# A chunked recurrence on one core: order of TensorE's and VectorE's work around the scans

## The chip, the cores and the metric

The kernel runs on one core of a Trainium2 chip. Its time is the device time of one execution in microseconds, and the number quoted for a kernel is the median of its runs. The profile is of one execution on the same core, with its own time. The engines are TensorE (PE, its weight loads PEld), VectorE (DVE), ScalarE (ACT), GpSimd (POOL) and SyncE (SP, which starts DMAs). They run side by side, each works through its own list in order, and they meet in semaphores.

## The reference

One block of a hybrid network over 2048 tokens of 256 numbers: a gated recurrence with rotations, a mixture of 8 experts, a windowed attention, and the mixture again. The change lies in the recurrence alone:

```python
q = causal_conv(ln(x) @ Wq); k = causal_conv(ln(x) @ Wk); v = causal_conv(ln(x) @ Wv)   # 4 taps each, 6 heads of 64
theta = q[..., ::2] * inv_freq; psi = k[..., ::2] * inv_freq
alpha = sigmoid(ln(x) @ Wa); beta = sigmoid(ln(x) @ Wb)
state = rotate(state, theta_t - theta_(t-1)) * alpha + beta * rotate(v, psi)            # over the tokens
out   = rotate(state, -theta)
g = ln(x) @ Wg
o = out * rsqrt(mean(out**2) + eps) * rms_w * silu(g)
x = x + o @ Wo
```

Turning the state into a frame that rotates with theta makes the recurrence a plain scan, `o = alpha * o + w`, with `w` the values turned by the angle psi - theta and scaled by beta.

## The kernel before, in words

The recurrence works on four chunks of 512 tokens. Features lie on the partitions, tokens along the row. All engines run one loop over the chunks, `it` = 0 to 3, and in turn `it` the outputs of chunk `it` are finished while chunk `it + 1` (`ahead`) is prepared up to its scans. What stands ahead of the loop prepares chunk 0. So there are three full turns, and a last one with outputs alone.

Preparing a chunk means, on TensorE: `angles` for two units of 128 features (24 matmuls of 512 columns each, L351, the taps folded into the weights), `decays` (six matmuls to 12 rows), three value projections and three gate projections (`value_or_gate`, six matmuls each, L362), then `betas` and `alphas` (L386 to L394), which spread the decays over the partitions. Angles, values and gates share one PSUM tensor of two banks, `psV`; each projection waits until ScalarE has copied out the one that held its bank. ScalarE rounds the angles (`rounded`, L515), VectorE subtracts (`start`, L675), and only then may values overwrite the bank. ScalarE copies values out (`values_out`, L529), takes sines (`turns`), and Silu of the gates (L544). VectorE convolves the values with four taps (`taps`, L725 for the first and L729 for the others), turns them (`rotate`), adds (`write`), scales by beta (`write_scaled`), and runs three scans (`scans`, L762), which start from the carried state `carry` of the chunk before (L765).

Finishing a chunk means: ScalarE squares the scans' outputs (L550), TensorE sums the squares by head (`squares`, 24 small matmuls to 6 columns, L403), ScalarE adds a constant (`means`, L555), GpSimd raises to the power -1/2 (`deviations`, L632, two instructions), TensorE spreads the result over the partitions (`rms_spread`, L413), VectorE multiplies it with the gated outputs (`outputs`, L777 and L774; the gating is GpSimd's, L625), and TensorE projects (`project_out`, L425). In the turn after that the result is added to x and normalised (`tail_stats_dve`, `tail_xn_dve`, with GpSimd's part `tail_pool`, TensorE's transposes L162 and ScalarE's copy), the logits of the experts follow (`routed_logits`, L997), VectorE picks two experts per token (`Routing`, in two parts: up to the picks, L1057 to L1076, and from the counts on, L1093 to L1113), TensorE counts (`pe_ranks`, which waits for the picks, L1023), and GpSimd sends the rows out (L1184). The first turn has no logits and picks; instead the last chunk's input is transposed and split into high and low parts there (L147), and the first projection waits for that split.

Nothing but the order of the calls in each engine's list sets the order of the work. After the four turns a barrier closes the recurrence (L180), and experts and attention follow in blocks of their own.

## Time and profile before

| | us |
|---|---|
| median of the runs | 772.26 (767.83, 772.26, 773.0) |
| profiled execution | 766.56 |
| its span, first to last instruction | 764.8 |
| TensorE busy | 618.8 (81%) |
| VectorE busy | 465.6 (61%) |
| ScalarE busy | 296.7 (39%) |
| GpSimd busy | 342.0 (45%) |

The shares are over the whole program. What concerns the recurrence is read from its own stretch, which ends 229 us into the span, by the timeline of each engine and by stretches cut at points of TensorE's order.

### The profile page before, as it was taken

The page shows a single profiled execution, that of the slowest core. Times are in us where ns is not written, and L with a number is a line of the kernel's source. Part 1 is how long each engine was busy: PE and PEld are TensorE (multiplying, and loading weights), DVE is VectorE, ACT ScalarE, POOL GpSimd, SP SyncE. Part 2 cuts the span into 40 slices and gives each one's busy share as a digit, 9 for nine tenths or more (in the row PEclk, how much of TensorE's full clock was granted, in tenths as well). Part 3 has the DMA queues.
Part 4 walks back from the last instruction along what each step waited for, and adds up shares of the span by engine and source line. Part 5 has one row for each costly group of instructions (what it writes and reads, how often), then busy time and mean ns, then how long its engine had stood idle before and what let it go on. Part 6 is the DMA issues. An engine that isn't in the chain of part 4 may idle for free. (4 is left out here: it accounts for less than half of the span.)

```text
span 764.8 us, 14771 instructions
## 1 busy us (share of the span) xinstructions
PE 618.8 (81%) x4827; PEld 479.8 (63%) x4827; DVE 465.6 (61%) x1226; ACT 296.7 (39%) x567; POOL 342.0 (45%) x400
## 2 busy tenths in 40 slices
PE   1789999995639999964569999999988769999950
PEld 0667787774535767743457787877866545777740
DVE  6994858869435534456365766787786544644422
ACT  1363435152002444444134545555454413444420
POOL 4304040723531667755332444345557650653435
PEclk9998989896666999986658999999999756999985
DMA  8599500132011453327435246403501512443328
GB/s 274 201 351 351 184 1 0 45 90 74 22 61 56 145 168 98 100 79 239 62 69 85 57 105 150 95 24 78 107 17 46 135 53 58 145 135 100 99 93 295
DMA packets 68318, 86.94 MB, mean 114 GB/s; under 512 B 8909, under 2 KB 62802, under 8 KB 67380
## 3 DMA queue, kind: packets, MB, share of 16 engines
q1 hardware_dynamic: 61428, 67.80, 32.7%
q0 software_dynamic: 6816, 18.19, 6.7%
q8 instruction: 42, 0.69, 0.4%
q14 instruction: 32, 0.26, 0.1%
HBM read 35.13 MB, written 39.06 MB: 97 GB/s over the span
## 5 line engine op out<-in xcount | busy, mean ns | idle before, releaser
L1295 POOL DMA_INDIRECT back<-f_yout,f_target x78 | 76.9, 985 | 113.2 <-ACT f_yout L1402 102.6
L1337 PE MATMUL bank<-f_wgu,f_xt 128*128 x312 | 113.5, 488 | 3.4 <-ACT f_xt L1387 3.3
L1184 POOL DMA_INDIRECT xs<-xn,f_slots x64 | 65.2, 1018 | 57.3 <-ACT xn L1175 41.7
L1442 DVE TENSOR_TENSOR f_hid<-f_act_g,bank 128x176 f32<-128x176 f32 x78 | 26.4, 338 | 104.3 <-ACT f_act_g L1394 100.2
L1359 PE MATMUL bank<-f_wd,f_hT 88*128 x312 | 81.5, 385 | 0.0
L2069 POOL TENSOR_SCALAR_AFFINE_SELECT b_prob<-b_prob 128x512 f32<-128x512 f32 x60 | 38.4, 640 | 92.6 <-ACT b_prob L2310 92.3
L2310 ACT ACTIVATE b_prob<-bank 128x1024 f32<-128x1024 f32 x60 | 61.5, 1024 | 46.2 <-PE bank L2149 45.9
L1337 PEld LDWEIGHTS bank<-f_wgu,f_xt 128*128 128x128 f32 x312 | 59.2, 199 | 31.1 <-issue 9.4
L2379 DVE COPY_PREDICATED bank<-b_later,bank 128x512 f32<-128x512 int32 x60 | 41.6, 694 | 33.5 <-PE bank L2119 30.1
L1359 PEld LDWEIGHTS bank<-f_wd,f_hT 88*128 88x128 f32 x312 | 54.2, 193 | 4.8
L1402 ACT ACTIVATE f_yout<-bank,f_share 128x256 f32<-128x256 f32 x78 | 37.0, 474 | 39.8 <-PE bank L1359 38.9
L1394 ACT ACTIVATE f_act_g<-bank 128x176 f32<-128x176 f32 x78 | 24.8, 318 | 66.7 <-PE bank L1337 66.7
L2190 PE MATMUL bank<-b_prob,b_V 128*17 128x128 f32 x992 | 42.0, 288 | 9.1 <-POOL b_prob L2071 8.5
L2383 DVE TENSOR_REDUCE b_m<-bank 128x4 f32<-128x512 f32 x64 | 44.2, 691 | 8.2 <-PE bank L2110 6.1
L2071 POOL TENSOR_SCALAR_AFFINE_SELECT b_prob<-b_prob 128x512 f32<-128x512 f32 x64 | 41.0, 641 | 11.5 <-ACT b_prob L2307 11.5
L2149 PE MATMUL bank<-b_QS,b_KS 64*128 64x128 f32 x496 | 41.5, 276 | 1.0 <-ACT b_prob L2310 0.7
L1387 ACT ACTIVATE f_xt<-bank 128x256 f32<-128x256 f32 x78 | 30.0, 384 | 25.9 <-PE bank L1321 17.6
L2149 PEld LDWEIGHTS bank<-b_QS,b_KS 64*128 64x128 f32 x496 | 36.5, 192 | 3.2 <-ACT b_prob L2310 2.0
L2119 PE MATMUL bank<-b_KS,b_QS 48*128 48x256 f32 x208 | 30.8, 343 | 8.1 <-DVE b_m L2383 8.1
L351 PE MATMUL bank<-xTh,wfh 128*128 128x512 f32 x64 | 30.1, 470 | 8.3 <-DVE wfl L705 8.3
L2190 PEld LDWEIGHTS bank<-b_prob,b_V 128*17 128x17 f32 x992 | 22.3, 99 | 20.8 <-POOL b_prob L2071 16.6
L1321 PE MATMUL bank<-ident_sb,f_xin 128*128 128x128 f32 x156 | 32.0, 289 | 1.4 <-DMA f_xin<-xs 1.4
(313 smaller groups left out, 1475.4 us busy)
## 6 DMA issues: line engine op xcount, KB each, us to landing
xs<-xTf SPq DMA_DIRECT2D x8, 2176.0 KB, 19.2
f_xin<-xs SPq DMA_DIRECT2D x78, 136.0 KB, 2.1
f_wgu<-in_wgu SPq DMA_DIRECT2D x4, 1408.0 KB, 6.0
f_wgu<-back SPq DMA_DIRECT2D x16, 256.0 KB, 5.6
b_KS<-b_kh SPq DMA_DIRECT2D x32, 128.0 KB, 4.1
b_QS<-b_qh SPq DMA_DIRECT2D x32, 128.0 KB, 3.8
f_back<-back SPq DMA_DIRECT2D x8, 512.0 KB, 8.5
f_wd<-in_wd SPq DMA_DIRECT2D x4, 968.0 KB
```

The source lines that it names most:

```text
L1184: pool.indirect_dma_start(m.xs, bass.IndirectOffsetOnAxis(m.slots[:, g, c, i:i + 1], 0), xn[:, g * TPC + i], None)\
L1295: pool.indirect_dma_start(m.back, bass.IndirectOffsetOnAxis(target[:, g % AR:g % AR + 1], 0), yout[:, g % YB], None, bounds_check=2 * 2 * ...
L1337: mm = pe.matmul(psG[:, g % 2, 0:2 * FH], xt[:, g % 2, k * P:(k + 1) * P], m.gu[:, k, bass.ds(e, 2 * FH)], start=k == 0, stop=k == KD - 1)
L1359: mm = pe.matmul(psY[:, g % 2, 0:D], hT[:, g % 2, k * P:(k + 1) * P], m.wd[:, k, bass.ds(e, D)], start=k == 0, stop=k == 1)
L1402: act.activation(yout[:, g % YB], psY[:, g % 2, 0:D], ACT.Copy, scale=share[:, g % AR:g % AR + 1])\
L2069: pool.affine_select(halves_of[:, :, 0], halves_of[:, :, 0], [[0, 4], [-1, P]], ALU.is_gt, 0.0, base=0, channel_multiplier=1)
L2071: pool.affine_select(halves_of[:, :, 1], halves_of[:, :, 1], [[0, 4], [1, P]], ALU.is_ge, 0.0, base=0, channel_multiplier=-1).then_inc(kep ...
L2149: mm = pe.matmul(own_t[:, half, i, w], KS[rows, 2 * u + i, ring(b - 1 + w)], QS[rows, 2 * u + i, ring(b)], start=True, stop=True)
L2190: mm = pe.matmul(psO[CG * j:CG * j + HV1, u * P:(u + 1) * P], V[:, (b - 1 + w) % RING, 4 * u + j], prob[:, quad(b, u) % 2, half, c:c + P], ...
L2310: ins = act.activation(dst, psT[:], ACT.Exp, scale=SCALE)
L2379: dve.copy_predicated(own_s[:, :, :, 1], later[:].unsqueeze(1).unsqueeze(1).broadcast_to([P, 2, 2, P]), own_s[:, :, :, 0]).then_inc(sel_do ...
L2383: dve.tensor_reduce(mo[:, :, 2 * u:2 * u + 2], own_s[:, :, :, 1], AX.X, ALU.max).then_inc(m_done, 1)
```

## The change

On TensorE, both angle units of the next chunk come before the squares, and its three values directly behind them; two of the three gates come before the projection. On ScalarE, copying the carried state is new work behind the squares; the rounding of the next angles moves ahead of the means, the values' copies ahead of the transposed rows, and of the three gates one precedes the copy of the counts. On VectorE, the copy of the carried state is gone, the taps run value by value instead of tap by tap and stand before the outputs instead of behind them (the last tap no longer behind the picks), `start` precedes the normalisation, and `rotate` follows the picks instead of the second part of the routing. GpSimd's list and the DMAs keep their order.

```diff
@@ -468,9 +468,11 @@
                     ahead = it + 1 < NCH
                     if ahead:
                         angles(it + 1, 0)
+                        angles(it + 1, 1)
                     squares(it)
                     if ahead:
-                        angles(it + 1, 1)
+                        for i in range(VT):
+                            value_or_gate(it + 1, i)
                     if it == 0:
                         first_transposed(3)
                     else:
@@ -480,17 +482,15 @@
                     rms_spread(it, 0)
                     if ahead:
                         rms_spread(it, 1)
-                        value_or_gate(it + 1, 0)
-                        value_or_gate(it + 1, 1)
-                        value_or_gate(it + 1, 2)
                     if it > 0:
                         routed_logits(it - 1)
                     if ahead:
+                        value_or_gate(it + 1, VT)
+                        value_or_gate(it + 1, VT + 1)
                         project_out(it)
                         if it > 0:
                             pe_ranks(pe, m, 0, it - 1, psB[:, 0])
-                        for i in range(VT, NVG):
-                            value_or_gate(it + 1, i)
+                        value_or_gate(it + 1, VT + 2)
                         if it > 0:
                             pe.wait_ge(m.route, routed(0, it - 1, COPIED))
                         betas(it + 1)
@@ -537,9 +537,13 @@
                     act.activation(angle[:, 0], angle[:, 0], ACT.Sin, scale=-TWO_PI)
                     act.activation(angle[:, 1], angle[:, 1], ACT.Sin, scale=sscale[:, 0:1]).then_inc(sin_ready, 1)
 
-                def gates(it):
+                def carried(it):
+                    act.wait_ge(scan_done, now(it, GT, GT))
+                    act.activation(carry[:], o[:, :, CH - 1], ACT.Copy).then_inc(carry_done, 1)
+
+                def gates(it, which=range(VT, NVG)):
                     act.wait_ge(o2_ready, before(it, NOUT, NOUT))
-                    for i in range(VT, NVG):
+                    for i in which:
                         act.wait_ge(vg_ready, now(it, i + 1, NVG))
                         act.activation(gate[:, i - VT], psV[:, i % 2], ACT.Silu).then_inc(vg_out, 1)
 
@@ -575,9 +579,12 @@
                 gates(0)
                 for it in range(NCH):
                     squares(it)
+                    if it + 1 < NCH:
+                        carried(it)
+                        rounded(it + 1)
                     means(it)
                     if it + 1 < NCH:
-                        rounded(it + 1)
+                        values_out(it + 1)
                     if it == 0:
                         tail_act(act, t0, 3)
                     else:
@@ -586,12 +593,12 @@
                         tail_rows_act(act, tl, it - 1)
                     if it + 1 < NCH:
                         sigmoids(it + 1)
-                        values_out(it + 1)
                         turns(it + 1)
+                        gates(it + 1, [VT])
                     if it > 0:
                         act_counts(act, m, 0, it - 1, psB[:, 0])
                     if it + 1 < NCH:
-                        gates(it + 1)
+                        gates(it + 1, range(VT + 1, NVG))
                     if it > 0:
                         act_tanh(act, m, xn, 0, it - 1)
                 tail_rows_act(act, tl, NCH - 1)
@@ -717,18 +724,18 @@
                     dve.tensor_tensor(wgl[:], wg_raw, wgh[:].bitcast(F32), ALU.subtract).then_inc(wgl_done, 1)
                     dve.tensor_tensor(wof[:], wo_raw, rmsw[:].unsqueeze(2).broadcast_to([P, GT, D]), ALU.mult).then_inc(wgl_done, 1)
 
-                def taps(it, j):
-                    for i in range(VT):
+                def taps(it, i):
+                    for j in range(TAPS):
                         src = vraw[:, i, PAD - TAPS + 1 + j:PAD - TAPS + 1 + j + CH]
                         if j == 0:
                             dve.wait_ge(vg_out, now(it, i + 1, NVG))
                             dve.tensor_scalar(vconv[:, i], src, convv[:, i, 0:1], None, ALU.mult)\
                                .then_inc(tap_done, 1)
                         else:
-                            dve.wait_ge(tap_done, now(it, (j - 1) * VT + i + 1, NTAP))
+                            dve.wait_ge(tap_done, now(it, i * TAPS + j, NTAP))
                             dve.scalar_tensor_tensor(vconv[:, i], src, convv[:, i, j:j + 1], vconv[:, i],
                                                      ALU.mult, ALU.add).then_inc(tap_done, 1)
-                    if j == TAPS - 1:
+                    if i == VT - 1:
                         dve.tensor_copy(vraw[:, :, 1:PAD], vraw[:, :, CH + 1:CH + PAD]).then_inc(halo_done, 1)
 
                 def rotate(it):
@@ -761,9 +768,8 @@
                     for g in range(GT):
                         dve.tensor_tensor_scan(o[:, g], psF[:, g // 2], w[:, g], carry[:, g:g + 1],
                                                ALU.mult, ALU.add).then_inc(scan_done, 1)
-                    dve.wait_ge(scan_done, now(it, GT, GT))
-                    dve.tensor_copy(carry[:], o[:, :, CH - 1]).then_inc(carry_done, 1)
                     if it == NCH - 1:
+                        dve.wait_ge(scan_done, now(it, GT, GT))
                         dve.wait_ge(vg_out, now(it, NVG, NVG))
                         dve.tensor_tensor(gate[:], gate[:], o[:], ALU.mult).then_inc(gated, GT)
 
@@ -799,8 +805,8 @@
                 tail_xn_dve(dve, t0, 3)
                 tail_split_dve(dve, t0, 1)
                 dve.wait_ge(wgl_done, 2)
-                for j in range(TAPS):
-                    taps(0, j)
+                for i in range(VT):
+                    taps(0, i)
                 rotate(0)
                 write(0)
                 write_scaled(0)
@@ -811,26 +817,27 @@
                         tail_split_dve(dve, t0, 2)
                     else:
                         tail_stats_dve(dve, tl, it - 1, add=True)
-                        tail_xn_dve(dve, tl, it - 1)
                     if ahead:
                         start(it + 1)
+                    if it > 0:
+                        tail_xn_dve(dve, tl, it - 1)
                     if it == 0:
                         m.prepare(dve, xn)
+                    if ahead:
+                        for i in range(VT):
+                            taps(it + 1, i)
                     outputs(it, 0)
                     if ahead:
                         outputs(it, 1)
                     if it == 0:
                         tail_split_dve(dve, t0, 3)
-                    if ahead:
-                        for j in range(TAPS - 1):
-                            taps(it + 1, j)
                     if it > 0:
                         group = Routing(dve, m, 0, it - 1)
                         group.take(psB[:, 0, LOGITS])
                         group.compare()
                         group.choose()
                     if ahead:
-                        taps(it + 1, TAPS - 1)
+                        rotate(it + 1)
                     else:
                         outputs(it, 1)
                     if it > 0:
@@ -839,7 +846,6 @@
                         group.difference()
                         group.payload(xn)
                     if ahead:
-                        rotate(it + 1)
                         write(it + 1)
                         write_scaled(it + 1)
                         scans(it + 1)
```

How that stands in the lists, first on TensorE, around the squares (L403) of the second turn; L351 is an angle matmul, L362 with `wvh` and `wvl` one of a value, and the weights `wfh` and `wfl` are the high and low halves. Before:

```order
L351 MATMUL bank1<-xTl,wfh 128x512
L403 MATMUL bank2<-headsum,sq 128x6 x12
L351 MATMUL bank1<-xTh,wfh 128x512
L351 MATMUL bank1<-xTh,wfl 128x512
L351 MATMUL bank1<-xTl,wfh 128x512
```

And with the change:

```order
L351 MATMUL bank1<-xTl,wfh 128x512
L403 MATMUL bank2<-headsum,sq 128x6 x12
L362 MATMUL bank1<-xTh,wvh 128x512
L362 MATMUL bank1<-xTh,wvl 128x512
L362 MATMUL bank1<-xTl,wvh 128x512
```

The 24 matmuls of the second angle unit have moved from behind the squares to ahead of them, and the values now follow the squares with nothing in between.

On VectorE, the second turn from the end of the scans (L762) to the picks (L1076; with the change the line numbers are a few higher). Before:

```order
L765 COPY carry<-o 128x3
L130 TENSOR_TENSOR x_tok<-bank,x_tok 128x1024
L133 BN_STATS stats<-x_tok 128x6 x4
L136 BN_AGGR meanvar<-stats 128x2 x4
L142 TENSOR_SCALAR xn<-x_tok,meanvar,rstd 128x256 x4
L675 SCALAR_TENSOR_TENSOR angle<-whole,bank 128x1024
L777 TENSOR_TENSOR sq<-gate,bank 128x1024
L774 TENSOR_TENSOR sq<-gate,bank 128x512
L725 TENSOR_SCALAR vconv<-vraw,convv 128x512 x3
L729 SCALAR_TENSOR_TENSOR vconv<-vraw,convv,vconv 128x512 x6
L1057 COPY f_L<-bank 128x32
```

And with the change:

```order
L136 BN_AGGR meanvar<-stats 128x2 x4
L682 SCALAR_TENSOR_TENSOR angle<-whole,bank 128x1024
L142 TENSOR_SCALAR xn<-x_tok,meanvar,rstd 128x256 x4
L732 TENSOR_SCALAR vconv<-vraw,convv 128x512
L736 SCALAR_TENSOR_TENSOR vconv<-vraw,convv,vconv 128x512 x3
...
L739 COPY vraw<-vraw 128x3x3
L783 TENSOR_TENSOR sq<-gate,bank 128x1024
L780 TENSOR_TENSOR sq<-gate,bank 128x512
L1063 COPY f_L<-bank 128x32
```

The pair L732 and L736 stands there three times in a row, once per value; the dots stand for its second and third time. All twelve taps and the copy of the last columns (L739) now precede the outputs (L783, L780), and the picks begin behind those.

## Rows read from the trace of the kernel before

**Rows 1.** Stretches between the alphas' ends: bounds and length in us, engines' busy times, TensorE's clock.

```profile
core 0: us, PE busy (x) PEld busy (x) DVE busy (x) ACT busy (x) POOL busy (x), PEclk, DMA share, GB/s
53.30:92.89 39.59, 37.92 (x220) 29.88 (x219) 26.55 (x38) 15.98 (x21) 9.54 (x6) 0.91 0.95 294
92.89:134.37 41.48, 39.57 (x243) 31.54 (x242) 29.76 (x60) 16.59 (x24) 10.82 (x8) 0.92 0.00 1
134.37:178.03 43.66, 40.11 (x243) 31.74 (x242) 34.36 (x63) 16.58 (x24) 19.39 (x17) 0.92 0.27 72
```

**Rows 2.** Waits of TensorE, 53 to 187 us: total, times, longest.

```profile
PE bank L403 <- ACT sq L550: 9.6, 3, 7.2
PE bank L1023 <- DVE f_pick L1076: 2.6, 2, 1.3
PE bank L362 <- ACT gate L544: 1.9, 3, 0.6
```

**Rows 3.** Stretches of TensorE alone: length, busy time, granted clock, DMA.

```profile
60.06:63.74 3.68, 3.56 (x24) 0.84 1.13 350
63.74:71.95 8.21, 8.21 (x25) 0.66 1.13 352
92.89:100.11 7.22, 7.22 (x25) 0.76 0.00 0
100.11:102.71 2.60, 2.60 (x26) 1.00 0.00 0
102.71:109.92 7.21, 7.21 (x27) 0.76 0.00 1
134.37:140.20 5.83, 5.83 (x25) 1.00 0.20 75
141.68:145.26 3.58, 3.40 (x24) 0.89 0.22 80
145.26:153.66 8.40, 8.40 (x26) 0.64 0.00 0
```

**Rows 4.** Timeline: the carry copy in two turns, and GpSimd's gating beside the first.

```profile
142.51 3.72 POOL L625 TENSOR_TENSOR gate<-gate,o 128x512 f32<-128x512 f32 x3
143.28 2.98 DVE L765 COPY carry<-o 128x3 f32<-128x3 f32 x1
...
186.99 0.17 DVE L765 COPY carry<-o 128x3 f32<-128x3 f32 x1
```

**Rows 5.** First taps and fold products (ns min/median/max, first and last start); GpSimd's subtraction.

```profile
L725 DVE TENSOR_SCALAR vconv<-vraw,convv x12: 486/486/900, 40.8 to 163.0; 128x512 f32<-128x512 f32 x12
...
L695 DVE TENSOR_TENSOR f_wgu<-f_wgu,w x2: 693/1225/1757, 11.6 to 12.2; 128x512 f32<-128x512 f32 x2
...
40.18 1.28 POOL L619 TENSOR_TENSOR sgl<-sg,sgh 12x512 fp32r<-12x512 f32 x1 [1.60 <-ACT sgh L523]
```

**Rows 6.** Timeline of GpSimd, first turn: the power for the scales.

```profile
64.29 4.52 POOL L632 TENSOR_TENSOR rms<-ms,minus_half 128x16 f32<-128x16 f32 x2 [1.23 <-ACT ms L555]
```

**Rows 7.** Timeline of VectorE: outputs and split (first turn), taps and routing (second).

```profile
75.46 1.22 DVE L777 TENSOR_TENSOR sq<-gate,bank 128x1024 f32<-128x1024 f32 x1 [0.51 <-PE bank L413]
...
77.20 1.22 DVE L147 TENSOR_TENSOR xTl<-bank,xTh 128x1024 fp32r<-128x1024 f32 x1
...
116.56 0.49 DVE L725 TENSOR_SCALAR vconv<-vraw,convv 128x512 f32<-128x512 f32 x1 [1.31 <-ACT vraw L529]
...
119.68 4.06 DVE L729 SCALAR_TENSOR_TENSOR vconv<-vraw,convv,vconv 128x512 f32<-128x512 f32 x6
123.66 0.18 DVE L1057 COPY f_L<-bank 128x32 f32<-128x32 f32 x1
...
126.83 2.08 DVE L729 SCALAR_TENSOR_TENSOR vconv<-vraw,convv,vconv 128x512 f32<-128x512 f32 x3
```

**Rows 8.** Timeline of TensorE, second turn: first value matmul, logits, projection.

```profile
114.17 0.50 PE L362 MATMUL bank<-xTh,wvh 128*128 128x512 f32 x1
...
118.45 1.85 PE L997 MATMUL bank<-f_wr_raw,xTf 128*128 128x8 f32 x16
...
120.15 5.43 PE L425 MATMUL bank<-wof,sq 128*128 128x256 f32 x24
```

## The prediction, written before the run

> **What bounds the kernel now.** I read the table of stretches first. The recurrence fills the first 229 of 764.8 us; the change touches nothing behind it, and a barrier separates the two, so what the last chunk's scans gain arrives at the end of the program unchanged. Cut at the end of the alphas' matmuls, the three full turns of its loop take 39.59, 41.48 and 43.66 us, and TensorE is busy in 37.92, 39.57 and 40.11 of them; VectorE in 26.6 to 34.4 [rows 1]. So TensorE's order bounds the loop, and VectorE follows it. What is not plain matmul work on TensorE has two sources.
>
> First, its waits [rows 2]: 9.6 us for the squares, of which 7.2 lie behind the last turn, so 2.4 here; 2.6 for the routing's picks; 1.9 for a gate's bank. In the chunks whose squares arrive one by one the 24 small matmuls of that step take 3.68 and 3.58 us against 2.60 when all three are there [rows 3]: 2.1 more. Second, the granted clock. Twenty-four angle matmuls take 5.83 us at the full level (2.4 GHz), 5.6 up to the start of what follows, since the last one overlaps with it. Four stretches were partly at the lower level (1.2 GHz): 8.21, 7.22, 7.21 and 8.40 us at a mean clock of 0.66, 0.76, 0.76 and 0.64 [rows 3]. Three of them follow the squares, one the betas and alphas. They cost 2.6 + 1.6 + 1.6 + 2.8 = 8.6 us. Waits, slow squares and clock together are 2.4 + 2.6 + 1.9 + 2.1 + 8.6 = 17.6 us of the three turns.
>
> **The change part by part.** *TensorE.* Both angle units now run before the squares, 11.2 us of dense work. A turn's scans end 8.9 us behind the alphas (178.03 in [rows 1], 186.99 in [rows 4]), so the squares are all there: the 2.4 and the 2.1 go. Two gates move ahead of the projection and only the third follows; the picks and the gate's bank are then ready behind 5.4 us of projection [rows 8]: the 2.6 and the 1.9 go. The clock's 8.6 I count anew below.
>
> *Carry copy to ScalarE.* On VectorE it took 2.98 us in one chunk and 0.17 when nothing ran beside it [rows 4]. It is off the path: behind it VectorE waited in every turn for ScalarE's rounding, which waited for the angles on TensorE. On ScalarE it stands behind the squares and ahead of that same wait. Counted 0; should the angles stop being late, it is worth up to 2.8 us once.
>
> *ScalarE's and GpSimd's other steps.* The means wait for the squares on TensorE wherever they stand; the transposed rows give way to the three values' copies, and the logits that need them come 5 us later on TensorE; sines and the first gate follow while VectorE still has taps, outputs and picks to do. Counted 0; without that cover a late sine holds the rotation, which is the second rival. GpSimd's list keeps its order; where its sends stand ahead of the gating (from 142.51, when the scans were nearly over [rows 4]) the power may begin up to 1 us later, which goes into the range. SyncE's loads of expert weights wait for the last angles and values and start some us earlier, with nobody waiting: 0.
>
> *Taps by value.* Taps that don't depend on each other start every 0.66 us (4.06 for six less 2.08 for three, over three) though each lasts 0.76 [rows 7]. By value each waits for the one before, so nine cost at least 0.76 each, 6.8 us, and the three first ones 0.49 each [rows 5]: 8.3 us. That is about 0.8 more per chunk, and is in the chain below. The three chunks' extra increments and the tap order of chunk 0, ahead of the loop, I count as 0: VectorE's next work there waits for betas and alphas on TensorE.
>
> *A new wait.* Here is the step that decides. Before, the taps came long after GpSimd's power for the scales; now the values follow the squares directly on TensorE, and ScalarE has the first one out about 2.4 us after them (values start at 114.17 on TensorE, the first tap at 116.56; [rows 7, 8]). GpSimd's power starts 0.55 us behind the squares (63.74 in [rows 3], 64.29 in [rows 6]) and lasts 4.52, to 5.1 us behind them. The first tap of a value is a one-input VectorE operation like the carry copy, and both wait for GpSimd: the carry copy issued at 143.28, inside GpSimd's three products, ended at 146.26, with the last of them at 146.23 [rows 4]; the first tap that met GpSimd's 1.28 us subtraction at 40.18 took 0.90 instead of 0.49 [rows 5]. So I let the first tap wait for the whole power. The bounds are no wait (2.4 us) and the whole of it (5.1 us); the carry copy is the nearest row, and I take 5.1.
>
> From the end of the squares, VectorE then needs 5.1 + 8.3 + 0.2 (halo) + 1.7 (outputs, 75.46 to 77.20) = 15.3 us until the outputs are written, and in the first turn 1.2 more, since the projection also waits for the last split [rows 7]. TensorE is at the projection after the values 4.3, transposes, decays and the spread of the scales 4.25 (109.92 to 114.17), logits 1.7 and two gates of 1.43, a third of the values' time, = 13.1 us, in the first turn 11.4 without logits [rows 3, 8]. **It waits 5.1, 2.2 and 2.2 us, 9.5 in all.** A slow clock behind the squares, 1.6 to 2.8 us as before, fits into these waits and costs nothing on top. That is the trade: the old stalls give way to one before the projection.
>
> The Trainium skill, page "SBUF — State Buffer", section "SBUF: two separate sides", speaks against the change here too, but more mildly: such a VectorE operation and a GpSimd instruction lock each other out for one whole instruction. This trace shows more than that: the carry copy stayed out over three GpSimd instructions in a row. By the page the tap would come in between the two power instructions and the sum would be about 4.5 us better, 762, the first rival below; I go by the row.
>
> *Clock, what stays.* Waiting 5 us before the first projection probably lowers the clock under it. Bounds: 0, and 2.6 as for the angles behind the idle and squares of the first turn; I take 1.5. One fall behind betas and alphas in three turns, as before: 1.6 (bounds 0 and three at 1.6).
>
> *Sum.* Removed 17.6; added 9.5 + 1.5 + 1.6 = 12.6; the last alphas end 5.0 us earlier. From the outputs to the end of the scans VectorE needs 19.6 us (123.66 to 143.28) less three taps and the halo, 2.1 = 17.5 [rows 4, 7]. From the projection to the alphas TensorE needs 14.2 (120.15 to 134.37) less the 1.9 of waits and two gates 2.9 = 9.4 [rows 1, 8]. The scans thus end 8.1 behind the alphas, against 8.9: another 0.8. **Gain 5.8 us.** Behind the scans the order is as before. The profiled execution, 766.56 us, becomes 760.8. The runs shown are 767.83, 772.26 and 773.0, so the profiled one lies 5.7 under their median; I take the median's side: 772.26 - 5.8 = **766 us** (766.46, rounded down). By the runs' own spread, 1% (7.7 us) is about what a measurement of this kernel can tell from no change.
>
> **Rivals.** *The taps don't wait, or less.* If the first tap comes in between the power's two instructions, of which the second handles 8 of 24 columns and so takes about a third, an estimate of 1.5 us, the waits shrink by 1.5 in each turn: 766 - 4.5 = 762. With no wait at all VectorE is done at 12.5 us, TensorE never waits outside the first turn, and the clock may hold: 17.6 and 0.8 gained and about 2 added, 756. For it: operations with two inputs did get in between GpSimd's products, 1.76 us against 0.69 alone [rows 5]. Against it: the carry copy did not. Chance 0.25.
>
> *It is all given back.* VectorE's work from the squares to the outputs is longer than I count (the subtraction on GpSimd, 1.28 us, falls among the taps and holds one of them; ScalarE's sines come late for the rotation), by some 2 us a turn: 766 + 6 = 772. For it: VectorE has no slack left in that stretch. Chance 0.20.
>
> *Slower: the cold projection.* In each turn the wait before the projection lets the clock fall, and projection, gate, betas and alphas hold it down into the next angles. That makes 2.7 of cold angles and 1.5 of cold projection three times, 12.6 instead of the 3.1 I counted; 9.5 more: 766 + 9.5 = 776, and with the projections at their bound of 2.6 each 779. It decides where the wait is long enough for a fall in all three turns, not in the first alone. For it: betas and alphas preceded a fall once (92.89 in [rows 3]) without any long wait. Against it: the turn with 1.28 us of waiting before the picks shows no fall behind its alphas (134.37, clock 1.00), and what comes before the projection is dense. Chance 0.10.
>
> The forecast has what is left, 0.45. Its own range is 763 to 770 by the bounds of clock and first wait. For 8 in 10 I go from 758, inside the case without waits, to 774, inside the given-back case and noise of the median. Faster by over 1% means under 764.5: the first rival and a part of the forecast, 0.25 + 0.09 = 0.34. Slower by over 1% means over 780: the third rival's end together with the runs' spread, 0.06. Within 1%: 0.60.
>
> **What would show it.** In the profile after: squares in 2.6 us with no wait before them; the first tap of each chunk starting where the power on GpSimd ends, or, if that step is wrong, some 2.4 us behind the squares; TensorE's idle before the projection 5, 2 and 2 us, named after the outputs on VectorE; no idle before picks and gates; the scans of the last chunk at 181 instead of 187. Taps at 0.77 to 0.79 us a step. Wrong would be angles at a mean clock under 0.8 in all turns, or VectorE idle before the rotation for the sines.

## The result and the profile after

The changed kernel takes 757.61 us (756.68 to 759.75, four runs) against 770.35 us of the kernel before in four (767.83, 768.44, 772.26, 773.0), 12.7 us between the medians. A ratio, here and below, is taken from runs in the faster of two states alone, so it need not be the quotient of the medians (0.983): it is 0.988, interval 0.9835 to 0.9929. That is 1.2% faster, just past the 1% that the prediction called "within", and the median lies 0.4 us below the low end of its range. With more runs (12 and 23, first experiment on the other parts) the ratio is 0.992 (0.987 to 0.997), 6.2 us less on 770.62, close to the 5.8 us forecast. By these the size was met. The way to it was not: the step on which the sum turned did not happen.

The profiled execution took 759.75 us, its span is 758.0 us, 6.8 shorter than the one before. First the stretches between the alphas' ends (as in [rows 1]: length, busy times of the engines, TensorE's clock):

```profile
55.61:96.65 41.04, 37.91 (x219) 30.05 (x219) 27.52 (x36) 16.19 (x22) 9.82 (x6) 0.91 0.85 265
96.65:134.75 38.10, 37.98 (x243) 30.59 (x243) 29.41 (x56) 16.40 (x23) 11.06 (x8) 0.96 0.00 1
134.75:172.86 38.11, 37.95 (x243) 30.55 (x242) 32.84 (x62) 16.90 (x25) 19.98 (x16) 0.96 0.32 82
```

The three turns take 117.25 us instead of 124.73. In the second and third TensorE is idle for 0.1 to 0.2 us: nothing but its own work sets them. TensorE's waits from 53 to 187 us, beside [rows 2]:

```profile
PE bank L403 <- ACT sq L554: 6.6, 1, 6.6
PE bank L425 <- issue: 3.1, 1, 3.1
PE bank L425 <- DVE sq L780: 0.2, 1, 0.2
```

Those for picks and for a gate's bank are gone, the 6.6 for the squares lie behind the last turn. In front of the projection (L425) stands 3.1 us in the first turn and 0.2 behind, where the sum had 5.1, 2.2 and 2.2. TensorE alone (as in [rows 3]):

```profile
55.61:68.78 13.17, 13.17 (x50) 0.84 1.13 352
68.78:71.49 2.71, 2.71 (x26) 1.00 1.13 351
...
86.16:92.92 6.76, 6.76 (x25) 0.75 0.09 28
96.65:109.44 12.79, 12.79 (x49) 0.87 0.00 0
...
134.75:147.54 12.79, 12.79 (x49) 0.87 0.18 67
```

The rows are: both angle units of the first turn, its squares, its projection, and the angles of the second and third turn. Squares now take 2.7 us in each turn, without a wait (predicted 2.6). The angles (11.26 us for both units at the full level, shown below) lose 1.9, 1.5 and 1.5 us to the low clock, and the projection loses 1.7 (5.07 at the full level, below). And the step itself, on GpSimd and VectorE in the second turn:

```profile
112.58 4.72 POOL L639 TENSOR_TENSOR rms<-ms,minus_half 128x16 f32<-128x16 f32 x2 [6.78 <-ACT ms L559]
121.15 1.29 POOL L626 TENSOR_TENSOR sgl<-sg,sgh 12x512 fp32r<-12x512 f32 x1 [3.86 <-ACT sgh L523]
...
114.52 0.49 DVE L732 TENSOR_SCALAR vconv<-vraw,convv 128x512 f32<-128x512 f32 x1 [1.22 <-ACT vraw L529]
115.04 2.33 DVE L736 SCALAR_TENSOR_TENSOR vconv<-vraw,convv,vconv 128x512 f32<-128x512 f32 x3
...
120.56 3.22 DVE L736 SCALAR_TENSOR_TENSOR vconv<-vraw,convv,vconv 128x512 f32<-128x512 f32 x3
...
123.77 1.21 DVE L783 TENSOR_TENSOR sq<-gate,bank 128x1024 f32<-128x1024 f32 x1
```

The squares end at 112.15. The first tap starts at 114.52, 2.4 us behind them, in the middle of the power, and takes its usual 0.49; it had waited for ScalarE's copy of the value alone. The three taps behind it, with two inputs each, take 2.33 us inside the power. The third value's three taps take 3.22 us, beside GpSimd's subtraction; so it is in all three turns of this trace.

### The profile page after: what moved, and what is told of

Read it like the earlier page. It is cut to its first block and busy times, and to the rows that moved or that the text cites. A ratio compares the mean times of both kernels' runs of the same rounds, so it can differ in the third digit from the quotient of the medians.

```text
span 758.0 us, 14773 instructions
## 1 busy us (share of the span) xinstructions
PE 617.0 (81%) x4827; PEld 479.6 (63%) x4827; DVE 467.2 (62%) x1222; ACT 297.2 (39%) x570; POOL 343.8 (45%) x400
## 5 line engine op out<-in xcount | busy, mean ns | idle before, releaser
L2077 POOL TENSOR_SCALAR_AFFINE_SELECT b_prob<-b_prob 128x512 f32<-128x512 f32 x64 | 40.9, 639 | 11.5 <-ACT b_prob L2313 11.5
L351 PE MATMUL bank<-xTh,wfh 128*128 128x512 f32 x64 | 28.6, 446 | 8.3 <-DVE wfl L712 8.3
L1353 PEld LDWEIGHTS bank<-ident_sb,f_hid 128*88 128x88 f32 x156 | 19.3, 125 | 21.6 <-issue 13.7
```

Of the source, the lines that this page charges most:

```text
L2077: pool.affine_select(halves_of[:, :, 1], halves_of[:, :, 1], [[0, 4], [1, P]], ALU.is_ge, 0.0, base=0, channel_multiplier=-1).then_inc(kep ...
```

## How the experiments are read

Where a kernel has six executions or more, they scatter by 11 to 20 us, and go with the mean granted TensorE clock that each lists: of 80 runs of the kernel before, the slowest has 779.31 us at 0.847 and the fastest 759.51 at 0.879. A line through all runs, with a constant for each kernel, falls by 4.9 us for 0.01 of clock and leaves 1.4 us. So the table gives, beside the median and the ratio to before on the same chip, the difference to before at equal mean clock, from that line and all runs, with its 95%. What an order gains or loses by raising or lowering the mean clock itself is not in that difference; whether any does was not separated (median clocks of the changed kernel and of before, first experiment on the other parts: 0.865 and 0.859). The other columns come from one trace each: the three turns between alphas, and TensorE's waits in them. The two kernels with probes or products ran once each, for their traces (770.51 and 778.52 us).

| kernel | median (runs) | ratio | at equal clock | turns | waits |
|---|---|---|---|---|---|
| before, second trace | 769.44 (8) | 0.999 (0.992 to 1.006) | 0 | 121.71 | 5.8 |
| changed, again | 764.22 (12) | 0.992 (0.987 to 0.997) | -4.8 ± 0.8 | 116.88 | 3.1 |
| outputs earlier, first turn | 760.13 (6), 757.03 (12) | 0.984 (0.972 to 0.995), 0.989 (0.985 to 0.993) | -9.7 ± 0.7 | 108.76, 111.74 | 0.2, 0.4 |
| outputs earlier, all turns | 758.16 (6) | 0.990 (0.981 to 0.998) | -9.1 ± 1.1 | 111.16 | 0.9 |
| carry copy on VectorE | 761.49 (12) | 0.993 (0.988 to 0.998) | -5.2 ± 0.8 | 117.36 | 3.3 |
| first tap waits | 768.71 (12) | 1.006 (1.001 to 1.011) | +3.2 ± 0.8 | 126.23 | 11.7 |
| gates late | 773.59 (6) | 1.012 (1.002 to 1.023) | +3.7 ± 1.1 | 134.25 | 14.1 |
| outputs before taps | 767.85 (12) | 0.998 (0.993 to 1.004) | -1.1 ± 0.8 | 119.81 | 8.0 |
| angles split | 777.81 (6) | 1.014 (1.003 to 1.025) | +4.6 ± 1.1 | 131.57 | 12.1 |

## Experiments on the step that failed

**The first tap made to wait.** What the prediction assumed, put in by hand:

```diff
                     if ahead:
+                        dve.wait_ge(rms_ready, now(it, NRMS, NRMS))
                         for i in range(VT):
                             taps(it + 1, i)
```

> The change with one wait added: the first tap of each chunk waits for the whole of GpSimd's power, which is the step that the prediction counted on and that the trace did not show. Theory A (the sum was right but for this step): the first tap moves from 2.4 to about 5.1 us behind the squares, TensorE's idle before the projection becomes 5.8, 2.8 and 2.8 us instead of 3.1, 0.2 and 0, and the time is 8 us above the changed kernel's at the same mean clock: nothing left of the gain, ratio to before 0.998 to 1.006. Rival B (the projection is not held by the taps): the time of the changed kernel, ratio 0.992.

The power and first tap of the first turn in that kernel, and TensorE's waits:

```profile
70.09 4.51 POOL L639 TENSOR_TENSOR rms<-ms,minus_half 128x16 f32<-128x16 f32 x2 [5.99 <-ACT ms L559]
74.64 0.49 DVE L732 TENSOR_SCALAR vconv<-vraw,convv 128x512 f32<-128x512 f32 x1 [4.68 <-POOL rms L639]
```

```profile
PE bank L425 <- issue: 5.9, 1, 5.9
PE bank L425 <- DVE sq L780: 5.8, 2, 3.0
```

The tap starts where the power ends, 5.0 us behind the squares (69.67), and the idle before the projection is 5.9 and twice 2.9, as expected. At equal clock the kernel is 8.0 us above the changed one, the ratio 1.006 at the edge of what was expected. Theory A stands: the projection hangs on the taps, and the sum's price for a held first tap was right (2.7 us a turn; the waits grow from 3.3 to 11.7). The hold was not there.

**What holds VectorE: probes.** A copy with the form of the carried state's stands ahead of the first tap, a tap-like operation where GpSimd gates; nobody reads either.

```diff
+                def probe_tap():
+                    dve.tensor_scalar(probe[:], o[:, 0], convv[:, 0, 0:1], None, ALU.mult)
+
+                def probe_copy():
+                    dve.tensor_copy(seen[:], sq[:, :, CH - 1])
...
+                    if it in (1, 2):
+                        probe_tap()
                     if ahead:
                         start(it + 1)
...
                         for i in range(VT):
+                            if i == 0:
+                                probe_copy()
                             taps(it + 1, i)
```

> The change with two probes on VectorE, whose results nobody reads: ahead of each chunk's first tap a copy of 128x3 values with the form of the copy of the carried state (so it meets GpSimd's power), and ahead of the subtraction of the angles in the second and third turn a tap-like operation (one input, 128x512; in the third turn it meets GpSimd's gating products). Theory A (what GpSimd runs decides: products of 128x512 hold VectorE out, the power on 128x24 values does not): the copy takes 0.17 to 0.2 us inside the power, the tap-like operation inside the gating takes over 1 us instead of 0.49. Rival B (what VectorE runs decides: a plain copy is held out, a tap with its scalar from memory is not): the copy inside the power takes 1.5 to 4.7 us, the tap-like operation 0.49 inside the gating.

The copy beside the power (second turn) and the tap-like operation beside the gating (third), from its timeline:

```profile
109.74 4.72 POOL L640 TENSOR_TENSOR rms<-ms,minus_half 128x16 f32<-128x16 f32 x2 [6.64 <-ACT ms L560]
110.38 0.16 DVE L746 COPY seen<-sq 128x3 f32<-128x3 f32 x1
...
142.05 3.76 POOL L633 TENSOR_TENSOR gate<-gate,o 128x512 f32<-128x512 f32 x3
143.01 3.09 DVE L743 TENSOR_SCALAR probe<-o,convv 128x512 f32<-128x512 f32 x1
```

The copy passes inside the power in 0.16 us; the tap-like operation takes 3.09 and ends behind the last product (0.46 in the second turn, outside the products). What GpSimd runs decides, not what VectorE runs: theory A. The carry copy of [rows 4] is no model for a tap beside the power, since its neighbour was another.

**Products in the power's place.** GpSimd computes three products of 128x512 into an unused place and then one product of the 128x24 values, instead of the power (so the scales are left out).

```diff
+                    if it + 1 < NCH:
+                        pool.wait_ge(wgl_done, 1)
+                        for n in range(3):
+                            pool.tensor_tensor(probe[:, n * KD:(n + 1) * KD], wgh[:, :, 0:2 * P].bitcast(F32), wgl[:, :, 0:2 * P].bitcast(F32), ALU.mult)
...
+                        if it + 1 < NCH:
+                            pool.tensor_tensor(by_h(rms), by_h(ms), by_h(minus_half), ALU.mult).then_inc(rms_ready, 1)
+                            continue
                         pool.tensor_tensor(by_h(rms), by_h(ms), by_h(minus_half), ALU.pow).then_inc(rms_ready, 1)
```

> The change with GpSimd's power replaced by three products of 128x512 values into an unused place and a product of the same 128x24 values (so the scales are not the right ones). Theory A (products of that size hold the first taps out, the power does not): the first tap, ready 2.4 us behind the squares, ends with the last of the products, some 4.4 us behind the squares, or is as long as one product, over 1 us, and TensorE's idle before the projection is 1 to 2 us longer in each turn than in the changed kernel. Rival B (the first tap gets in whatever GpSimd runs): 0.49 us at 2.4 us behind the squares, and the same idle as in the changed kernel.

First taps beside the products in the first and third turn, the normalisation beside them in the second, then TensorE's waits:

```profile
69.48 3.97 POOL L641 TENSOR_TENSOR probe<-wgh,wgl 128x512 f32<-128x512 f32 x3 [5.99 <-ACT ms L560]
71.41 0.90 DVE L740 TENSOR_SCALAR vconv<-vraw,convv 128x512 f32<-128x512 f32 x1 [2.06 <-ACT vraw L530]
...
109.33 3.40 DVE L142 TENSOR_SCALAR xn<-x_tok,meanvar,rstd 128x256 f32<-128x256 f32 x4
...
151.69 3.90 POOL L641 TENSOR_TENSOR probe<-wgh,wgl 128x512 f32<-128x512 f32 x3 [2.27 <-ACT ms L560]
...
154.36 1.52 DVE L740 TENSOR_SCALAR vconv<-vraw,convv 128x512 f32<-128x512 f32 x1
```

```profile
PE bank L426 <- issue: 4.6, 1, 4.6
PE bank L426 <- DVE sq L788: 4.1, 2, 2.1
```

The tap takes 0.90 and 1.52 instead of 0.49, the four operations of the normalisation 3.40 instead of 1.38, and TensorE idles 1.5 to 2 us longer in each turn: theory A again. Here the tap stays out for the product that runs (in the first turn it ends at 72.31, the products at 73.45); the probe above stayed out for the rest of three. The carry copy of the kernel before did both: 2.98 us in the third turn, but 0.28 and 0.34 in the first two, where it met the same three products (lines in the section on the prediction). The operations that stayed out for all (2.98, 3.09, and 2.97 in the second trace of before) are all in the third turn, where the products follow GpSimd's sends; whether that makes the difference is open.

## Experiments on the other parts

**The changed kernel again**, without an edit.

> The changed kernel once more, five rounds. Theory A (the gain is made in the three full turns, whose stretches shrank from 124.73 to 116.99 us, and TensorE's order sets it): 757 to 758 us, ratio about 0.983 to 0.988; in an execution whose gates of the first chunk, ahead of the loop, run at the high clock, the first alphas end at 53.3 instead of 55.6 us and the gain of the loop shows whole. Rival B (a good part of the 12.7 us between the medians is the difference between executions and not the change): ratio 0.99 or above.

The ratio, 0.992, is rival B's, its interval reaches down into theory A's. The turns, 116.88 us, are those of the first trace (117.25), as theory A has it; but part of the 12.7 us was the executions', as rival B has it. The first four runs of the changed kernel had clocks of 0.873 to 0.877; here its median clock is 0.865. The trace, of an execution with a mean clock of 0.849, shows the low clock elsewhere than in the first one; the rows are the first turn's angles and projection, the angles of the second turn, its values, the angles of the third, its values:

```profile
55.83:69.66 13.83, 13.83 (x50) 0.79 1.13 352
87.05:92.12 5.07, 5.07 (x25) 1.00 0.06 16
95.85:107.11 11.26, 11.26 (x49) 1.00 0.00 0
110.04:117.10 7.06, 7.06 (x20) 0.57 0.00 0
135.01:146.27 11.26, 11.26 (x49) 1.00 0.20 75
148.99:154.79 5.80, 5.80 (x20) 0.71 0.00 0
```

The same list of instructions, slow in the first turn's angles as in the first trace, but at the full clock in the projection and in the later angles, and slow in the values behind these (4.26 at the full level). Where the clock falls is not a property of the order alone.

**The kernel before again**, without an edit.

> The kernel before, unchanged, for a second trace of it. In the one trace shown the alphas of the first chunk end at 53.3 us, in nearly all traces with the change at 54.7 to 56.0, since the last gate there runs at the low clock. Theory A (which stretch runs at the low clock differs from one execution to the next, with either order): the first alphas end anywhere from 53.3 to 56 us; the three turns together again take 124 to 126 us. Rival B (the change itself costs those 2.3 us ahead of the loop, by its taps by value): 53.3 us again.

```profile
55.65:92.14 36.49, 35.86 (x219) 28.52 (x218) 25.11 (x36) 15.98 (x21) 9.56 (x6) 0.95 0.97 303
92.14:133.62 41.48, 39.58 (x244) 31.49 (x243) 29.76 (x60) 16.59 (x24) 10.81 (x8) 0.92 0.00 1
133.62:177.36 43.74, 40.19 (x243) 31.72 (x242) 34.42 (x63) 16.58 (x24) 19.47 (x17) 0.92 0.27 71
```

Its first alphas end at 55.65 now: theory A, the change costs nothing ahead of the loop. But the first turn is 3.1 us shorter than in [rows 1], below the 124 to 126 expected for the three, so one trace of each kernel tells the gain of the loop only to some 3 us: 4.8 us by the second pair (121.71 to 116.88), 7.5 by the first.

**The wait that was left.** In the first turn the outputs and the last split move ahead of the third value's taps.

```diff
                     if ahead:
-                        for i in range(VT):
+                        for i in range(VT if it > 0 else VT - 1):
                             taps(it + 1, i)
...
                         tail_split_dve(dve, t0, 3)
+                        taps(1, VT - 1)
```

> The change, but in the first turn the outputs and the last split stand ahead of the third value's taps. Theory A: TensorE's 3.1 us wait before the first projection goes, and with it most of the cold projection (7.1 against 5.45 us): 4 to 5 us less than the changed kernel, 753 us; the alphas of that turn end some 4.8 us earlier and everything behind follows. Rival B: the loop is held by something else in that turn (VectorE's products, which end at the same time as before, or a fall of the clock in another place): 0 to 2 us less, 756 to 758 us.

> The version with the outputs and the last split ahead of the third value's taps in the first turn, once more for its interval. Theory A: ratio to before 0.984 to 0.989, 4 us under the changed kernel at the same mean clock, TensorE without a wait before the first projection. Rival B: no better than the changed kernel, ratio 0.990 to 0.994.

The turns and the first projection in the first of the two runs:

```profile
54.88:88.97 34.09, 34.09 (x220) 27.48 (x219) 26.80 (x37) 16.19 (x22) 9.82 (x6) 1.00 1.05 327
88.97:125.53 36.56, 36.44 (x244) 29.39 (x243) 30.04 (x56) 16.40 (x23) 11.10 (x8) 1.00 0.00 1
125.53:163.64 38.11, 37.95 (x243) 30.55 (x242) 32.80 (x62) 16.90 (x25) 19.98 (x16) 0.96 0.31 82
```

```profile
80.25 5.34 PE L425 MATMUL bank<-wof,sq 128*128 128x256 f32 x24
```

TensorE is busy in 34.09 of 34.09 us, the projection starts without a wait and at full speed, and at equal clock the kernel is 4.9 us below the changed one over 18 runs: theory A, expected 4 to 5. It is faster than both kernels. In the second run's trace the first turn takes 36.90 us, again without a wait, at a mean clock of 0.92: the clock alone makes 2.8 us between two traces of one kernel.

**The same in all turns**, with the projection directly behind the logits in the later ones.

```diff
+                        if it > 0:
+                            project_out(it)
                         value_or_gate(it + 1, VT)
                         value_or_gate(it + 1, VT + 1)
-                        project_out(it)
+                        if it == 0:
+                            project_out(it)
...
-                        for i in range(VT):
+                        for i in range(VT - 1):
                             taps(it + 1, i)
...
+                    if ahead:
+                        taps(it + 1, VT - 1)
```

> As the run on the first turn, and in the other two turns as well the outputs stand ahead of the third value's taps, with the projection directly behind the logits and two gates behind it. Theory A, second part: the angles behind betas and alphas ran cold (6.4 us for 8 of 24 columns' groups, clock 0.73, 1.6 us lost each) because little dense work lay between the projection and them; with three gates there again they run at the high clock in two turns: 3.2 us less than the first-turn version, about 750 us. Rival B: the fall belongs to betas and alphas themselves, with 12 rows: the same time as the first-turn version, 753 us. The three taps that met GpSimd's subtraction (3.23 us) take 2.33 where they no longer meet it.

No better than the first turn alone (-9.1 against -9.7, within both intervals): the second part of theory A falls. Its angles did run in 11.26 us in the second and third turn, but so did those of the changed kernel in the trace above, and the third turn's values took 5.67 instead. The fall moved and was not saved. Rival B named the right time, but its reason (betas and alphas themselves) does not hold either. The subtraction now met a first tap instead:

```profile
114.91 1.26 POOL L629 TENSOR_TENSOR sgl<-sg,sgh 12x512 fp32r<-12x512 f32 x1 [3.86 <-ACT sgh L526]
...
115.53 0.93 DVE L735 TENSOR_SCALAR vconv<-vraw,convv 128x512 f32<-128x512 f32 x1
```

**Carry copy back on VectorE.**

```diff
-                        carried(it)
                         rounded(it + 1)
...
+                    dve.wait_ge(scan_done, now(it, GT, GT))
+                    dve.tensor_copy(carry[:], o[:, :, CH - 1]).then_inc(carry_done, 1)
```

> The change, with the copy of the carried state back on VectorE behind the scans. Theory A: VectorE waits 3 to 7 us for ScalarE's rounding behind it in every turn, so it is off the path: the same time as the changed kernel, within 1 us. Rival B: the copy is locked out by GpSimd's gating once or more (2.98 us in the kernel before) and delays statistics and normalisation: up to 3 us more, 760 us.

-5.2 against -4.8: nothing, as the prediction counted.

**Gates behind the projection again.**

```diff
-                        value_or_gate(it + 1, VT)
-                        value_or_gate(it + 1, VT + 1)
                         project_out(it)
...
-                        value_or_gate(it + 1, VT + 2)
+                        for i in range(VT, NVG):
+                            value_or_gate(it + 1, i)
...
-                        gates(it + 1, [VT])
...
-                        gates(it + 1, range(VT + 1, NVG))
+                        gates(it + 1)
```

> The change with all three gates behind the projection again (on ScalarE behind the counts again). Theory A: the two gates are the work that covers VectorE's taps and outputs; without them TensorE waits 6, 3 and 3 us before the projection, and about 0.6 per turn for a gate's bank: 9 to 10 us above the changed kernel at the same mean clock, ratio to before about 1.004. Rival B (the gates moved only to spare the waits for picks and bank, 4.5 us in the kernel before): 4 to 5 us above the changed kernel, ratio 0.998.

```profile
PE bank L425 <- issue: 6.1, 1, 6.1
PE bank L425 <- DVE sq L778: 6.1, 2, 3.1
PE bank L362 <- ACT gate L547: 1.9, 3, 0.6
```

Waits of 6.1, 3 and 3.1 as expected, and 8.5 us above the changed kernel at equal clock, where 9 to 10 was expected: theory A, a little oversized. The two gates matter as the work that covers VectorE's taps.

**Outputs before all taps again**, VectorE's order alone undone.

```diff
-                    if ahead:
-                        for i in range(VT):
-                            taps(it + 1, i)
                     outputs(it, 0)
...
                         tail_split_dve(dve, t0, 3)
+                    if ahead:
+                        for i in range(VT):
+                            taps(it + 1, i)
```

> The change with VectorE's outputs (and the last split) ahead of all taps again; TensorE's and ScalarE's order as in the change. Theory A: TensorE doesn't wait before the projection any more, but the taps then end 6 to 9 us later and hold the picks: TensorE waits some 3.7 us for them in the second and third turn, the last scans end about 5 us later than in the changed kernel: ratio to before 0.997 to 1.001. Rival B (TensorE's order alone carries the gain, VectorE's has slack): the time of the changed kernel or, by the first turn's wait that goes, 3 to 5 us less, ratio 0.985 to 0.992.

```profile
PE bank L1029 <- DVE f_pick L1082: 6.3, 2, 3.2
PE bank L362 <- DVE angle L682: 1.7, 2, 1.0
```

The projection no longer waits, the picks do, 3.2 and 3.1 us (expected 3.7). The last scans end 2.8 us later than in the changed kernel, counted from the first alphas (128.3 against 125.5 us), where about 5 was expected. Ratio 0.998, 3.7 us above the changed kernel at equal clock: theory A. TensorE's order without VectorE's keeps about a quarter of the gain (-1.1 ± 0.8 of -4.8).

**Second angle unit behind the squares again.**

```diff
                         angles(it + 1, 0)
-                        angles(it + 1, 1)
                     squares(it)
                     if ahead:
+                        angles(it + 1, 1)
...
                         carried(it)
-                        rounded(it + 1)
                     means(it)
                     if it + 1 < NCH:
+                        rounded(it + 1)
                         values_out(it + 1)
```

> The change with the second angle unit behind the squares again (on ScalarE the means ahead of the rounding again). Theory A: TensorE waits for the squares of the last scans again and takes them one by one, 1 to 2.5 us per turn, and the rest of the change keeps its gain: 3 to 5 us above the changed kernel at the same mean clock, ratio 0.996 to 0.999. Rival B (the pause at the squares also lets the clock fall behind them, as in the kernel before, 1.6 to 2.6 us per turn more than falls elsewhere): 8 to 11 us above, ratio 1.003 or more.

```profile
PE bank L362 <- DVE angle L682: 7.7, 3, 2.6
PE bank L425 <- issue: 2.7, 1, 2.7
PE bank L403 <- ACT sq L554: 1.7, 2, 0.9
```

9.4 us above the changed kernel, rival B's size, but in the main not its reason. The angle unit behind the squares does run cold in two turns (7.17 and 7.37 us instead of 5.6), but the changed kernel's angles lose as much in all; the waits, 12.1 us against 3.3, make 8.8 of the 9.4. The squares cost only 1.7 us of waiting. In each turn TensorE stands 2.6 us before the values, which may overwrite the angles' bank only when ScalarE has rounded and VectorE subtracted. In the changed kernel the squares (2.7 us) stand in that place and cover it. Neither theory had that wait. The values behind it ran at 5.8 us in each turn, slow.

## Why the prediction came out as it did, step by step

The sum turned on the first tap's meeting with GpSimd's power. The trace of the kernel before has two readings for it that the prediction doesn't name, here from the timelines of GpSimd and VectorE in its first and second turn:

```profile
59.34 3.72 POOL L625 TENSOR_TENSOR gate<-gate,o 128x512 f32<-128x512 f32 x3 [17.88 <-DVE o L762]
61.57 0.28 DVE L765 COPY carry<-o 128x3 f32<-128x3 f32 x1
...
104.40 4.52 POOL L632 TENSOR_TENSOR rms<-ms,minus_half 128x16 f32<-128x16 f32 x2
104.54 1.38 DVE L142 TENSOR_SCALAR xn<-x_tok,meanvar,rstd 128x256 f32<-128x256 f32 x4 [1.55 <-POOL rstd L156]
```

The carry copy that served as the price was the dearest of three beside the same products: in the first and second turn it got in behind the second product and took 0.28 and 0.34 us. And in the second and third turn four one-input operations of the normalisation run inside the power in 1.38 us; they take the same at 33.76, where GpSimd runs nothing.

- **"So I let the first tap wait for the whole power": failed.** It starts 2.4 us behind the squares, the lower bound. Of the two bounds I took the one whose row looked nearest by VectorE's side (a copy, one input). The probes and the products show that GpSimd's side decides, and by that side the rows above spoke against a hold by the power. The first rival had the step right, at 0.25 and with 756 us for no wait at all; in time the first four runs (757.61) lie nearer to it, the twelve (764.22) nearer to the forecast. The Trainium skill, page "SBUF — State Buffer", section "SBUF: two separate sides", gives the port pair that VectorE, in some of its operations, shares with GpSimd to whichever starts first, for its whole instruction. Where I set the row against it, both were off the mark for the power: 0.49 and 0.16 us inside 4.7 us of it show no lock at all. Where an operation stayed out for what was left of one product (0.28, 0.34, 0.90, 1.52) the runs agree with the page; the 2.98 and 3.09 over what was left of three go beyond it.
- **Waits before the projection, 9.5: measured 3.3.** VectorE's chain was right apart from that step: nine dependent taps and three first ones take 8.4 us (predicted 8.3) where nothing meets them, TensorE's way from the squares to the first projection 11.5 us (71.49 to 86.16 less the wait of 3.1; predicted 11.4). The subtraction among the taps, left to the second rival, costs 0.9 per turn (in the second trace in the first turn alone). With the hold put in, the waits are 11.7.
- **Clock that stays, 3.1: measured 6.7** (1.9 + 1.7 + 1.5 + 1.5 in the first trace, before rounding). I tied falls to places, behind the squares and behind betas and alphas, and let the waits swallow some. The waits did not come, and the second trace of the same kernel has most of the falls elsewhere. Added in all: 10.0 instead of 12.6 us. The first pair of traces gives 17.6 - 10.0 = 7.6 for the turns, and 7.5 is read there.
- **Removed, 17.6: right as a list** (no wait for squares in the turns, picks and bank, squares packed), but one trace's clock: the second trace of before has a shorter first turn by 3.1.
- **Counted at nothing:** the carry copy (shown by its experiment). Sines, means, sends and loads name no wait of TensorE in the trace after. One wait was never counted and never came: the 2.6 us per turn for rounding and subtraction ahead of the values, which the squares cover. The scans' lag is 8.2 us (181.08 less 172.86) against 8.1 predicted.
- **The number.** 5.8 us of gain against 6.2 (ratio 0.992) or 4.8 at equal clock: two errors, 6.2 too much for waits and 3.6 too little for the clock, largely cancel, so that the sum came near is in good part luck. So is the end of the last scans, foretold for 181 and read at 181.08: the loop gained 2.5 us more than summed, but its first alphas ended 2.3 us later than in the trace of before (55.61, 53.30). The base, 772.26 from three runs, was high: over 80 runs the median of before is 770.5. That, and the high clocks of the first four runs after, put their median below the range.

## What to carry to other kernels

When a row serves as the price of a meeting of two engines, look for one that matches on both sides, and at every place where the two meet; here the neighbour's work decided, not the operation that waited, and the trace before the change had rows that said so. Count for each engine the work from the same event to the same meeting point, as done here for squares to projection: that told which order is free and found the 4.9 us that the change had left. Compare orders by waits, and times at equal clock, before a few us of difference between two medians are believed.

## What the runs showed of the hardware that was not expected

- GpSimd's power on 128x16 and 128x8 values, 4.7 us long, let VectorE's operations through at full speed, with one input (0.49, 0.16, four in 1.38) and with two (three taps in 2.33); its products of 128x512 kept the one-input kinds out for 0.1 to 2.8 us. Whether the size or the operation makes the difference was not separated.
- A subtraction of 12x512 on GpSimd (1.3 us) delays VectorE's two-input taps, too, by 0.9 us in each turn where it meets them.
- The low clock falls on the later angles in one execution and on the values in another of the same program, and the time follows the mean clock by 4.9 us for 0.01.
